# Side matmuls of a fused attention and expert kernel: a written table of turns replaced by a rule that spaces them

## The reference, cut to what matters

```python
q = _lora(x, Wq, Aq, Bq) ...            # x @ W.T + x @ Bm.T @ A.T * 2, same for k and v
s = einsum('bhqd,bhkd->bhqk', q, k) / sqrt(16) + slopes * (i - j)
s = where(j <= i, s, -1e30)
out = einsum('bhqk,bhkd->bhqd', softmax(s), v) @ Wp.T
x = _layernorm(x + out)
probs = softmax(x @ Wg); topv, topi = top_k(probs, 2)
pos = place of each (token, choice) in its expert, counted in the order of the tokens
h = gelu(expert_in @ W1 + b1); y = h @ W2 + b2   # up to cap rows per expert
x = _layernorm(x + sum of the two gated rows of y)
```

## Time and profile before

| | us |
|---|---|
| median of 3 runs | 1287.51 |
| lowest and highest | 1286.75, 1291.27 |
| the profiled execution, its own time | 1286.75 |
| its span, first to last instruction | 1285.0 |

### The profile page before, as it was taken

How to read it: one execution, slowest core, us unless ns; L and a number is a source line. 1 busy time by engine, 2 the same in 40 slices (tenths; PEclk the granted TensorE clock), 3 DMA queues, 4 the chain that set the end, 5 groups by cost and what they waited for, 6 DMA issues and landing times. The chain is left out here.

```text
span 1285.0 us, 24471 instructions
## 1 busy us (share of the span) xinstructions
PE 1157.6 (90%) x8759; PEld 503.9 (39%) x8759; DVE 627.0 (49%) x1751; ACT 916.6 (71%) x1203; POOL 354.7 (28%) x382
## 2 busy tenths in 40 slices
PE   7899999999999999999999899229999999999990
PEld 4322222222222222222222111117787787787770
DVE  4544342132365354725444101627757657658746
ACT  2799999999999999899999997125435435435314
POOL 2421111111141303213132200142552552552440
PEclk9999999999999999999999999559999999999995
DMA  6941322323330322223030000633423523421216
GB/s 151 201 109 56 98 74 63 72 71 91 77 108 21 111 46 87 69 60 98 30 89 20 23 3 10 203 102 110 114 34 111 127 23 108 119 29 15 27 22 261
DMA packets 83745, 104.22 MB, mean 81 GB/s; under 512 B 14937, under 2 KB 68932, under 8 KB 83632
## 3 DMA queue, kind: packets, MB, share of 16 engines
q1 hardware_dynamic: 66512, 77.74, 21.4%
q0 software_dynamic: 15744, 23.83, 8.8%
q10 hardware_dynamic: 1376, 1.18, 0.7%
HBM read 56.99 MB, written 48.29 MB: 82 GB/s over the span
## 5 line engine op out<-in xcount | busy, mean ns | idle before, releaser
L1358 ACT ACTIVATE prob<-ps_s 128x1024 f32<-128x1024 f32 (+3 forms) x854 | 716.9, 977 | 42.5 <-PE ps_s L1259 41.7
L1276 PE MATMUL ps_o<-prob,v_aug 128*17 128x512 f32 (+3 forms) x3294 | 428.3, 568 | 4.8 <-POOL prob L1384 2.3
L1259 PE MATMUL ps_s<-qop,kop 51*128 51x512 f16 (+3 forms) x1647 | 265.8, 368 | 22.2 <-ACT prob L1358 8.9
L1259 PEld LDWEIGHTS ps_s<-qop,kop 51*128 51x128 f16 x1647 | 63.5, 93 | 396.9 <-ACT prob L1358 379.7
L2104 PE MATMUL ps_y<-w2s,hs 128*128 128x256 bf16 (+1 forms) x1728 | 199.5, 273 | 1.2 <-DVE yb L2181 1.2
L2151 ACT ACTIVATE hid<-ps_h,b 128x384 f32<-128x384 f32 (+1 forms) x192 | 105.1, 560 | 118.8 <-PE ps_h L2088 94.5
L2088 PE MATMUL ps_h<-xs,w1s 128*128 128x384 bf16 (+1 forms) x1152 | 181.4, 317 | 5.0 <-ACT hid L2151 4.2
L1384 POOL TENSOR_SCALAR_AFFINE_SELECT prob<-prob 128x256 f32<-128x256 f32 (+1 forms) x180 | 69.6, 397 | 392.7 <-ACT prob L1358 390.2
L2104 PEld LDWEIGHTS ps_y<-w2s,hs 128*128 128x128 bf16 (+1 forms) x1728 | 167.4, 99 | 19.0 <-DVE yb L2181 1.5
L1420 DVE COPY acc<-ps_o 32x512 f32<-32x512 f32 (+2 forms) x105 | 72.1, 687 | 200.1 <-PE ps_o L1276 198.6
L2045 POOL DMA_INDIRECT result<-y,entry x72 | 111.9, 1555 | 179.6 <-DVE y L2186 149.9
(11 more groups left out here) (160 smaller groups left out, 713.7 us busy)
## 6 DMA issues: line engine op xcount, KB each, us to landing
w<-in_W SPq DMA_DIRECT2D x16, 1024.0 KB, 7.5
slots_x<-empty POOLq DMA_DIRECT2D x12, 520.0 KB, 3.8
qop<-fparts_q SPq DMA_DIRECT2D x42, 128.0 KB, 4.6
xe<-slots_x SPq DMA_DIRECT2D x8, 650.0 KB
x_all<-in_xT SPq DMA_DIRECT2D x8, 512.0 KB, 5.2
attnT<-acc SPq DMA_DIRECT2D x128, 32.0 KB
aT<-attnT SPq DMA_DIRECT2D x16, 256.0 KB
x_all<-in_x SPq DMA_DIRECT2D x8, 512.0 KB
```

What stands on the lines that cost most here:

```text
L1259: mm = pe.matmul(ps_s[:, u.p % SLOTS_S, e, a.q0:], o.key(e, a.h, a.kt), o.query(e, a.h, a.b, a.q0), start=True, stop=True)
L1276: mm = pe.matmul(ps_o[32 * c:32 * c + VW, a.q0:], o.v[:, a.kt, a.h], prob[:, t % RING, c % 2, c // 2, a.q0:], start=a.first, stop=a.last)
L1358: act.activation(prob[:, t % RING, n, e:z, q0:], ps_s[:, u.p % SLOTS_S, e:z, q0:], ACT.Exp, scale=1.0 / (SCALE * SCALE)).then_inc(exp_done, 1)
```

## The change

The table is dropped. Two rules stand in its place. `projections` gives each half, norm and value a last turn (the halves nine turns ahead of the first turn of their block, its norm seven, its values three ahead of its first diagonal turn) and spaces the pieces evenly up to it. `free_turn` puts each route, count, setup and bound on the first turn from a given one on that is free and has free neighbours. The steps of the choice follow the last route as before. Names that hang on the tables (`SCALE_AT`, `CHOOSE_AT`, `SPLIT_AT`, `GATE_AT`, `SCATTER_AT`, `FLAG_TURN`) follow the new turns. The pieces themselves, their number and all waits are the same.

```diff
-HALF_AT = {2: (6, 8, 10, 12, 16, 18, 22, 26),
-           3: (45, 47, 50, 54, 57, 59, 62, 66),
...
-ROUTE_AT = {0: (162, 166, 170, 173),
...
-COUNT_AT = {0: 186, 1: 216, 2: 250, 3: 276, 4: 310, 5: 337, 6: 368}
...
+def projections():
+    due = []
+    for n in range(2, NB):
+        due += [(FIRST_TURN[n] - 9, ("half", n, k, h)) for k in range(4) for h in range(2)]
+        due += [(FIRST_TURN[n] - 7, ("norm", n))]
+        due += [(DIAG_TURN[n] - 3, ("value", n, s)) for s in range(KT)]
+    due.sort(key=lambda d: d[0])
+    at, begin, i = {}, 5, 0
+    while i < len(due):
+        z = min(range(i, len(due)), key=lambda z: ((due[z][0] - begin) / (z + 1 - i), -z))
+        for k in range(i, z + 1):
+            at[begin + (due[z][0] - begin) * (k - i) // (z + 1 - i)] = due[k][1]
+        begin, i = due[z][0], z + 1
+    return at
+
+PIECE_AT = projections()
+
+def free_turn(t, piece):
+    while any(k in PIECE_AT for k in (t - 1, t, t + 1)):
+        t += 1
+    PIECE_AT[t] = piece
+    return t
...
+BOUND_TURN = free_turn(max(PIECE_AT) + 3, ("bound",))
+SETUP_TURN = free_turn(60, ("setup",))
 for _n in range(NB - 1):
...
-    for _s, _t in enumerate(ROUTE_AT[_n]):
-        SCALE_AT[_t - 2] = (_n, _s)
-    _t = ROUTE_AT[_n][-1] + 2
+    _t = _load + 10
+    for _s in range(KT):
+        SCALE_AT[_t] = (_n, _s)
+        _t = free_turn(_t + 2, ("route", _n, _s))
+    _t += 2
     for _k in range(CHOICES):
         CHOOSE_AT[_t + _k] = (_n, _k)
...
-    assert COUNT_AT[_n] >= _t + CHOICES
+    _t = free_turn(_t + CHOICES, ("count", _n))
```

More of the change, by code:

```diff
@@ L238 @@
-COUNT_AT = {0: 186, 1: 216, 2: 250, 3: 276, 4: 310, 5: 337, 6: 368}
[L239 to L251, removed]
+def projections():
[11 more added lines that the diff above has]
+        begin, i = due[z][0], z + 1
+    assert len(at) == len(due)
+    return at
@@ L277 @@
     SPREAD_AT[_load + 6] = _n
-    assert ROUTE_AT[_n][0] >= _load + 12
-    for _s, _t in enumerate(ROUTE_AT[_n]):
-        SCALE_AT[_t - 2] = (_n, _s)
-    _t = ROUTE_AT[_n][-1] + 2
+    _t = _load + 10
[3 more added lines that the diff above has]
+    _t += 2
     for _k in range(CHOICES):
@@ L286 @@
     GATE_AT[_t + 8] = _n
-    assert COUNT_AT[_n] >= _t + CHOICES
+    _t = free_turn(_t + CHOICES, ("count", _n))
     for _k in range(2 * KT):
-        SCATTER_AT[COUNT_AT[_n] + 2 + _k] = (_n, _k)
+        SCATTER_AT[_t + 2 + _k] = (_n, _k)
 assert len(LOAD_AT) == NB - 1 and len(SCALE_AT) == KT * (NB - 1) and len(CHOOSE_AT) == CHOICES * (NB - 1)
```

## The result

The changed kernel takes 1309.8 us (median of 4 runs, 1307.9 to 1310.6) against 1287.3 on the same chip: a ratio of 1.0172, 95% interval 1.0154 to 1.0190. I had forecast 1295.0 with a range up to 1303. The sign was right, the size far too small: 22.4 us lost, 7.5 forecast.

What follows compares the result with a forecast made beforehand. ACT was taken to bound the turns, with PE close behind. A 6.4, B 2.3 and C 0.1 made 8.8 us, 8.5 after overlap, on a profiled 1286.75: 1295.2, called 1295.0 us, range 1288 to 1303.

Steps and rivals of the forecast that it cites:

- A: Halves in narrow turns, 12 for 3 before, open idle time on ACT: 0.9 + 2.0 + 3.5 = 6.4 us.
- B: Values and routes in narrow turns or two turns behind another piece open more idle time on ACT: 2.3 us.
- overlap: Some of the terms' costs hide each other, such as a half in 225 and 274 hiding a late mask: 0.3 us off.
- C: Long waits of PE: new ones at counts, masks of 276 and turn 5's copy against old ones going: 0.1 us, bounds -6.0 to +6.
- The old waits: Waits at turns 276, 307, 183 and 249 go or shrink, 5.6 us together; 0.2 us more taken off in the sum.
- the six counts: Counts nearer the choice's first step: 0.7 to 1.2 us each on 249, 305, 336; 0.2 to 0.6 on 185, 216, 364.
- second rival: Choice too short for DVE: PE waits for the count while POOL's subtraction holds DVE, seven blocks, 7 us more, 1302 us; chance 0.15.
- third rival: DVE's copies start late behind a piece in the same turn, 0.2 us for each of 22 more: 4.4 more, 1299 us; chance 0.05.
- first rival: Pieces in first and third narrow turns cost nothing: A falls to 0.9, total 3.0 us, 1289.8 us; chance 0.20.
- the half in turn 5: At the start, it stands on DVE ahead of turn 5's copy, which comes a half's DVE work later: 1.2 us.
- The flag: Moves from turn 380 to 376, away from the narrow group at 382: called equal, with 0.4 us to gain.
- over 2 us: Sign that the forecast is wrong: a count waits that long.

Runs made afterwards that it cites:

- e12: Kernel before, with DVE's copy ahead of the turn's piece and POOL's split one turn behind the count, waiting for the end of `places`: ratio 0.9933, turns 752.8 us.
- e13: Changed kernel with DVE's copy ahead of the turn's piece and POOL's split waiting for the end of `places`: ratio to before 1.0079, turns 766.7 us.
- e6: Changed kernel with DVE's copy of the block's sums (evict) ahead of that turn's piece: ratio to before 1.0142, turns 775.1 us.
- e7: Kernel before with only counts moved earlier (185, 306, 335, 366 for 186, 310, 337, 368): ratio 1.0049, turns 762.8 us.
- e8: Changed kernel with POOL's split one turn behind the count and waiting for DVE's last sum of that block's choice: ratio to before 1.0132, turns 775.6 us.
- e9: Kernel before with only eight halves moved into narrow turns (53, 65, 93, 107, 143, 225, 274, 302): ratio 1.0027, turns 762.5 us.
- e14: Changed kernel with copy ahead of the piece, split waiting for `places`, and eight halves moved out of narrow turns: ratio to before 1.0022, turns 764.1 us.
- e1: Changed kernel with the counts of blocks 0 to 4 and 6 moved two to five turns later, flag to 380: ratio to before 1.0096, turns 776.2 us.
- e3: Changed kernel with the counts later and eight halves moved out of narrow turns: ratio to before 1.0096, turns 769.1 us.
- e11: Kernel before with DVE's copy of the sums (evict) ahead of that turn's piece and choice step: ratio 1.0002, turns 758.4 us.
- e4: Changed kernel with POOL's split issued one turn behind the count, not six behind the choice's first step: ratio to before 1.0137, turns 776.7 us.

## Why the prediction was wrong

e12 and e13 have the same two edits and differ in the turns of the pieces alone. With them the 21.4 us come apart:

| | forecast | measured, us |
|---|---|---|
| A, halves | 6.4 | 7.7 |
| B, values and routes | 2.3 | 5.9 |
| overlap, norms and the rest | -0.3 | 0.4 |
| C, long waits, with the clock behind them | 0.1 | 7.5 |
| sum | 8.5 | 21.4 |

The first three are e13 less e12, by the turns of each piece and the one behind (14.0 in all). C is what the two edits take away: 12.8 in the changed kernel less 5.3 in the one before. Of the 12.8, 0.9 are turn 3, which comes and goes, and some 1.6 are the copies that e6 showed, so the waits for counts, copies and masks with the clock are nearer 5 us than 7.5. The old waits were read rightly, 5.6 and 0.2 forecast for 5.3; it is the new ones that I had at 5.9 for 12.8.

**C is the step that failed.** I wrote that for block 4 "the half that stood ahead of it (1.1 us) and most of the 1.63 us step go, so it is about in time now". The 1.63 us was not a price of that step: it was POOL's subtraction, which meets some step of DVE, and doesn't go when the steps move, as it moves with them. In the changed kernel it holds `counts` for 2.14 us in block 4 and the running sums in block 0 (three that take 0.55 us elsewhere take 2.57, beside 2.13 of POOL). With it inside, the choice can be late for a count eight turns on: e7 shows that for block 4 with only counts moved, and e8 that without the meeting all four waits go. In both kernels the subtraction holds some step of DVE in each of the seven blocks, for 0.31 to 2.14 us; which step decides. The two longest waits, 1.63 and 2.85 us, stand where it holds one of the last (the sums, `counts`); where it holds `gap`, early in the choice, they are 0, 0.69 and 1.01, and in block 3, where it holds a copy behind the last sum, there is none. I had put 2.8 + 1.2 us on the six counts and 0.7 on 276.

The rule I cited, the Trainium skill, "SBUF — State Buffer", section "Who interferes with whom", says that VectorE and GpSimd share a pair of ports that one of them holds for a whole instruction. This case agrees by 2.14, 2.11, 1.99, 1.63 and 1.61 us for operations of DVE that otherwise take 0.16 to 0.2, each ending within 0.05 us of POOL's; not every operation of DVE is held, as the last section shows. I had made it the second rival with 0.15, at 1 us for each block. Its mechanism was the right one. Its price was uneven, 0.7 to 2.9 us of PE's waiting in four blocks and none in the others. That its 7 us on top of my sum come near the 7.5 measured for C is partly luck, since the 7.5 have the clock, the copies and turn 3 in them. From its 1302 to 1309.8 the largest piece is B (3.6 us), then A (1.3).

**The clock was in no sum of mine.** At 305 PE waits 2.85 us, and turns 305 to 309 cost 2.2 + 1.6 + 0.3 + 0.3 = 4.5 us above the same turns in e13. Part of the 1.6 is the late copy (0.6 by e6). I had rows 9 in hand, the clock at the lower level behind the flag's wait of 2.98 us, and used them for the flag alone. They were a price to be set, with a chance, against any long wait of PE.

**B was mis-sized.** I read 0.19 and 0.36 us as idle time of ACT. The turn itself gets longer by more: in e12 a value or route turn most often takes 2.16 us when no piece is within two turns ahead, 2.31 two turns behind one (though some take 2.18), and up to 2.61 where the turn of that earlier piece has a copy of DVE as well, against 1.81 for a turn without. That is 0.35, 0.50 and 0.80 us. ACT in e13, a route in 255 and a value in 257, each 0.80:

```profile
509.21 3.78 ACT L1369 ACTIVATE prob<-ps_s 128x1024 f32<-128x1024 f32 x4 [0.67 <-PE ps_s L1270]
513.67 3.77 ACT L1369 ACTIVATE prob<-ps_s 128x1024 f32<-128x1024 f32 x4 [0.67 <-PE ps_s L1270]
```

The rows show 0.67 idle for a price of 0.80. Four exponentials, two turns, take 3.77 us here, and two turns without a break 3.62 (twice 1.81): the last exponential ahead of an idle time ends some 0.15 us later than the next would have followed it, and the listing counts that as work. To each idle time of such a turn 0.15 is to be added. The dear kind, 2.59 us or more, is there 3 times in e12 and 8 times in e13, six of these two or three turns behind a piece with a copy in its turn (178, 197, 255, 257, 319, 324). This looks like another remainder of the third rival; it was seen and not tested, and e6 did not make these turns shorter. And the two routes in third narrow turns (227, 352) cost 0.6 and 1.1.

**A was about right**, by two errors that cancel: each narrow place was cheaper than I took it (third turn 0.76 for 0.88, first 0.30 to 0.38 for 0.5, second 0.62 to 0.78 for 0.88), but of the halves that I called free 263 and 291, two turns behind a route, cost 0.46 each, and 14, a short turn of the group that is narrow only in part, 0.74. The first rival, free narrow turns, is out by e9 and e14.

**Of the smaller steps:** the half in turn 5 holds the copy, PE waits 1.54 us at 6 (e6 and e13: gone, 0.9 us); I had 1.2 for it with the others. The flag behaves as forecast, within 0.5 us. The mask wait at 276 is 1.0 us in its turn and 0.5 more at the half clock in 278, for my 0.7. The old waits at 276 and 307 did go, as forecast, but at both places a new one stands: the masks of 274 and 275 now wait for the split, and the count of 305 for the sums.

**What stays open.** Which wait brings the half clock I can't say from these kernels. The count waits of 2.42 to 2.92 us at 305 and 306 had it in all five kernels that have them, and the flag's waits of 2.98 to 3.61 us in thirteen kernels; but in e6 the flag's 3.05 us had none. The mask waits at 276 of 1.52 us in the changed kernel, 1.51 in e6 and 1.67 in e1 had it, while 2.16 and 1.95 in the kernel before and 2.25 in e3 had not. So the "over 2 us" in what I expected of e7 is no rule. The stretch at turns 2 and 3 comes and goes between executions with the same order there; that only kernels with the changed plan show it may be chance, and it was not tried apart.

## What to carry to other kernels

Before moving work on DVE, look for an operation that lasts ten times its kind, and for what of POOL ends with it. That duration belongs to the pair and stays when the steps move. In this kernel a wait that kept POOL's long operation out of the chain was the cure; a later place in POOL's order was none where POOL ran ahead. Price a long wait of PE with the clock that may stand behind it. And price a side job by how much longer its turn gets, not by the idle time that the listing prints ahead of the next instruction.

## What was not expected of the hardware

- An operation of DVE with a single input can be held as well as one with two: `chosen` (128x8, a cast) 1.63 us for 0.17, `keep` in e8 (128x8, a comparison) 1.61 us beside a subtraction of 2.14. The timeline of DVE, then of POOL, in e8, block 5:

```profile
666.88 1.61 DVE L1792 TENSOR_SCALAR keep<-pos 128x8 f32<-128x8 f32 x1
```

```profile
666.33 2.14 POOL L1836 TENSOR_TENSOR xsplit<-x_all,xsplit 128x1024 bf16<-128x1024 f32 x1
```

- Not every operation is held. In the same block of e8 `place`, with one input in PSUM, takes its usual 0.22 us inside the subtraction, in e13 a copy out of PSUM its usual 0.43; FIND_INDEX8 takes 0.15 inside it in the kernel before (the line under e11). The same was seen of MAX8, of the reduction `pos` beside POOL's cast, and of the reciprocal. The timeline of DVE in e8, then of POOL and of DVE in e13:

```profile
666.37 0.22 DVE L1788 TENSOR_TENSOR place<-hot,ps_r 128x64 f32<-128x64 f32 x1
```

```profile
666.00 2.13 POOL L1836 TENSOR_TENSOR xsplit<-x_all,xsplit 128x1024 bf16<-128x1024 f32 x1
```

```profile
666.56 0.43 DVE L747 COPY v_aug<-ps_r 128x256 f32<-128x256 f32 x1 [0.62 <-PE ps_r L608]
```

- POOL loses next to nothing by the meeting: its subtraction takes 2.12 to 2.20 us with DVE beside it and 2.12 to 2.14 in e12, where nothing of DVE is held by it. Its cast of the same rows, 1.03 to 1.04 us, holds DVE too: `gap` takes 0.88 us beside it in the kernel before, 0.16 in e12.
- The half clock stayed for 6.8 us at the 2.85 us of waiting at 305 (from 0.6 us before the wait's end), with PE busy in 4.00 of the 4.00 us shown, and for 3.5 us at the flag's 3.36. The same wait at 305 had 3.4 us of it in e4, and there turns 305 to 309 were 0.8 us shorter.
